# Softmax row sums in an attention kernel: five probability tiles summed by accumulating DMAs instead of by matrix multiplies

## The reference

```python
xn = _layernorm(x)                                  # x: (4, 2048, 512) float32
q = split(xn @ q_w.T + q_b) / sqrt(32)              # 16 heads of 32, per batch: 64 heads in all
k, v = split(xn @ k_w.T + k_b), split(xn @ v_w.T + v_b)
ctx = softmax(q @ k.T, axis=-1) @ v                 # scores of a head: 2048 x 2048
out = x + (ctx @ out_w.T + out_b) + tanh(xn @ weight @ aux_weight1 @ aux_weight2 + ffn_bias)
```

## Time and profile before

| | |
|---|---|
| median of 3 runs | 4641.23 us (4627.87 to 4641.38) |
| the profiled execution | 4647.09 us, its span 4645.3 us |
| busy share of the span | PE 98%, POOL 69%, DVE 63%, ACT 53% |
| granted PE clock, mean | 0.983 of full speed |
| DMA, 1000 to 4000 us | 20% of the 16 engines, 45 GB/s |

### The profile page before, as it was taken

One profiled execution on the slowest core, in us unless ns is written; L12 is line 12 of the kernel. 1 busy time (PEld: TensorE's weight loads), 2 busy tenths in 40 slices (PEclk: granted clock), 3 DMA queues, 4 the chain that ended last, 5 costly groups with the idle time before them and its releaser, 6 DMA issues.

```text
span 4645.3 us, 81083 instructions
## 1 busy us (share of the span) xinstructions
PE 4555.9 (98%) x23776; PEld 2481.1 (53%) x23776; DVE 2937.3 (63%) x4928; ACT 2460.2 (53%) x4517; POOL 3197.8 (69%) x863
## 2 busy tenths in 40 slices
PE   7999999999999999999999999999999999999999
PEld 5888888444444444444444444444444444444457
DVE  3434343777767776767676767777676767677524
ACT  1222221366666666666666666666666666666631
POOL 0222222588888888888888888888888888888830
PEclk9999999799999999999999999999999999999999
DMA  4444444211111111212211121111211222211157
GB/s 152 163 154 163 154 160 163 57 42 43 43 43 42 43 45 43 50 43 53 43 42 43 42 43 43 43 43 43 45 42 43 51 46 48 43 42 42 47 171 255
DMA packets 288290, 338.44 MB, mean 73 GB/s; under 512 B 169984, under 2 KB 171008, under 8 KB 275584
## 3 DMA queue, kind: packets, MB, share of 16 engines
q1 hardware_dynamic: 286384, 332.48, 26.3%
q10 hardware_dynamic: 1488, 0.79, 0.1%
HBM read 195.30 MB, written 137.36 MB: 72 GB/s over the span
## 4 chain that ended last, share of the span: by engine, by line
PE 76%; issue 3%; DVE 2%; ACT 1%; DMA 0%; ACTq 0%; DVEq 0%; SPq 0%
PE sm_bank L773 25%; PE st_bank L789 20%; PE pv_bank L795 20%; PE sum_bank L795 7%; PE sm_bank L190 3%; DVE part_max L714 2%; PE st_bank L190 1%; ACT probs L645 1%; PE sm_bank L782 0%; DMA q_stack<-max_row 0%; DVE k_stack L728 0%; DMA s_sums<-sum_copy 0%; DVE probs L736 0%; DMA sums_col<-s_sums 0%; ACT q_stack L663 0%
## 5 line engine op out<-in xcount | busy, mean ns | idle before, releaser
L714 DVE TENSOR_REDUCE part_max<-sm_bank 128x1 f32<-128x512 f32 x4096 | 2502.2, 682 | 904.4 <-PE sm_bank L773 903.8
L612 POOL TENSOR_TENSOR pool_sum<-pool_sum,probs 128x2048 f32<-128x2048 f32 x576 | 2637.0, 4578 | 474.1 <-ACT probs L645 451.0
L645 ACT ACTIVATE probs<-st_bank 128x512 f32<-128x512 f32 x4096 | 2183.0, 604 | 1102.3 <-PE st_bank L789 1065.2
L773 PE MATMUL sm_bank<-k_stack,q_stack 96*128 96x512 f32 x4096 | 1849.7, 455 | 38.7 <-issue 17.4
L789 PE MATMUL st_bank<-q_stack,k_stack 97*128 97x512 f32 x4096 | 1651.4, 404 | 15.2 <-ACT probs L645 11.0
L773 PEld LDWEIGHTS sm_bank<-k_stack,q_stack 96*128 96x128 f32 x4096 | 782.6, 191 | 990.9 <-DVE part_max L714 622.6
L795 PE MATMUL pv_bank<-probs,v_head 128*32 128x512 f32 x8192 | 1029.8, 603 | 0.0
L789 PEld LDWEIGHTS st_bank<-q_stack,k_stack 97*128 97x128 f32 x4096 | 783.4, 191 | 160.1 <-ACT probs L645 73.3
L795 PEld LDWEIGHTS pv_bank<-probs,v_head 128*32 128x32 f32 x8192 | 214.4, 109 | 494.1 <-issue 370.1
L612 POOL TENSOR_TENSOR pool_sum<-probs 128x2048 f32<-128x2048 f32 x64 | 293.4, 4585 | 143.5 <-ACT probs L645 143.5
L795 PE MATMUL sum_bank<-probs,ones_att 128*32 128x512 f32 x2560 | 338.1, 600 | 0.0
(11 more groups left out here) (84 smaller groups left out, 2034.7 us busy)
## 6 DMA issues: line engine op xcount, KB each, us to landing
q_stack<-s_q_hi SPq DMA_DIRECT2D x128, 256.0 KB, 4.6
k_stack<-s_k_hi SPq DMA_DIRECT2D x128, 256.0 KB, 6.1
x_in<-in_x SPq DMA_DIRECT2D x16, 1024.0 KB, 7.7
s_q_hi<-qk_hi SPq DMA_DIRECT2D x16, 1024.0 KB, 4.3
s_q_lo<-qk_lo SPq DMA_DIRECT2D x16, 1024.0 KB, 6.4
s_k_hi<-qk_hi SPq DMA_DIRECT2D x16, 1024.0 KB, 4.3
s_k_lo<-qk_lo SPq DMA_DIRECT2D x16, 1024.0 KB, 6.4
s_v<-v_out SPq DMA_DIRECT2D x16, 1024.0 KB, 4.3
```

Of the source, the lines that this page charges most:

```text
L612: nc.gpsimd.tensor_tensor(total[:], one[:], probs[kt % PROBS][:], ALU.add).then_inc(pool_added, 1)
L645: nc.scalar.activation(probs[kt % PROBS][:, q * BLK:(q + 1) * BLK], st_bank[:, st_place(kt * QB + q)], ACT.Exp, scale=SCALE).then_inc(prob ...
L714: nc.vector.tensor_reduce(part_max[:, k:k + 1], sm_bank[:, sm_place(sm_slot(k))], AX.X, ALU.max).then_inc(max_scores_read, 1)
L773: nc.tensor.matmul(sm_bank[:, sm_place(sm_slot(k))], q_st[r][0:ROWS, q * P:(q + 1) * P], k_st[r][0:ROWS, b * BLK:(b + 1) * BLK], start=Tru ...
```

## The change

The five tiles that PE summed become `DMA_TILES` 1, 4, 7, 10, 13. SP copies the first of them into a new SBUF tile `dma_sum` (`first_tile`), and POOL issues four DMAs that add the others to it in place (`join`, `accum_op=ALU.add`), after its adds 2, 4, 6 and 8; each waits until the one before has landed (`joined`). PE sums `dma_sum` and `pool_sum` with ones in `add_up`, once a head, after tile 5 of the next head (`CUT` 6, it was 4). The bank of the sums becomes one turn in the ring of the maxima, which has four banks (`SM_BANKS`). POOL's first add now takes tiles 0 and 2, and `scale` comes after the seventh add (`SCALE_ADD` 7, it was 6). `RECIP_UNIT` moves from 48 to 56.

```diff
-BANKS = 3
+SM_BANKS, ST_BANKS = 4, 3
-RECIP_UNIT = 48
-CUT = 4
-DIRECT = [2, 5, 8, 11, 14]
-POOL_TILES = [kt for kt in range(KT) if kt not in DIRECT]
+SUM_UNIT = 40
+RECIP_UNIT = 56
+CUT = 6
+DMA_TILES = [1, 4, 7, 10, 13]
+POOL_TILES = [kt for kt in range(KT) if kt not in DMA_TILES]
+JOINED = (len(DMA_TILES) - 1) * DMA
+JOIN_AFTER = {2: 1, 4: 2, 6: 3, 8: 4}
-SCALE_ADD = 6
+SCALE_ADD = 7
...
+SM_TURN = [*range(TURN_UNIT), "max", *range(TURN_UNIT, SUM_UNIT), "sum", *range(SUM_UNIT, UNITS), None, None]
...
+            def first_tile(h, r):
+                sp.wait_ge(probs_ready, PRIME + h * UNITS + QB * (DMA_TILES[0] + 1))
+                sp.dma_start(dma_sum[r % 2][:], probs[DMA_TILES[0] % PROBS][:]).then_inc(first_copied, DMA)
...
                 if more >= 1:
                     load_row(following, (r + 1) % GROUP)
+                    first_tile(following, (r + 1) % GROUP)
...
+            def join(h, r, j):
+                if j == 1:
+                    pool.wait_ge(first_copied, PRIME + h * DMA + DMA)
+                else:
+                    pool.wait_ge(joined, h * JOINED + (j - 1) * DMA)
+                pool.sem_inc(join_due, 1)
+                nc.gpsimd.dma_start(dma_sum[r % 2][:], probs[DMA_TILES[j] % PROBS][:],
+                                    accum_op=ALU.add).then_inc(joined, DMA)
...
+            def sum_up(h, r, i):
+                add(h, r, i)
+                if i in JOIN_AFTER:
+                    join(h, r, JOIN_AFTER[i])
...
                         if old in POOL_TILES:
                             act.wait_ge(pool_added, PRIME + h * POOL_ADDS - back * POOL_ADDS + adds_after(old))
+                        elif old == DMA_TILES[0]:
+                            act.wait_ge(first_copied, PRIME + h * DMA + DMA)
+                        elif not (back and isinstance(h, int) and h == 0):
+                            act.wait_ge(joined, h * JOINED - back * JOINED + DMA_TILES.index(old) * DMA)
...
-                last = spread(pv_bank, v_sb[r][:, kt], tile, kt == 0, kt == KT - 1)
-                if kt in DIRECT:
-                    if kt == DIRECT[0]:
-                        pe.wait_ge(sums_copied, PRIME + h)
-                    last = spread(sum_bank, ones[:], tile, kt == DIRECT[0], False)
-                last.then_inc(tile_used, 1)
-            def add_partial(h, r):
+                spread(pv_bank, v_sb[r][:, kt], tile, kt == 0, kt == KT - 1).then_inc(tile_used, 1)
+            def add_up(h, r, more):
+                if more >= 2:
+                    pe.wait_ge(max_scores_read, PRIME + h * UNITS + 2 * UNITS + sm_before("sum")[0] + 1)
+                pe.wait_ge(joined, h * JOINED + JOINED)
+                spread(sum_bank, ones[:], dma_sum[r % 2], True, False)
                 pe.wait_ge(pool_added, PRIME + h * POOL_ADDS + POOL_ADDS)
                 spread(sum_bank, ones[:], pool_sum[r % 2], False, True).then_inc(sums_ready, 1)
```

More of the change, by code:

```diff
@@ L38, with sm_place, sm_before @@
 AHEAD = 4
-TURN_SLOT = 8
-RECIP_UNIT = 48
-CUT = 4
-DIRECT = [2, 5, 8, 11, 14]
-POOL_TILES = [kt for kt in range(KT) if kt not in DIRECT]
+TURN_UNIT = 8
+SUM_UNIT = 40
[3 more added lines that the diff above has]
+POOL_TILES = [kt for kt in range(KT) if kt not in DMA_TILES]
 POOL_ADDS = len(POOL_TILES) - 1
-SCALE_ADD = 6
+JOINED = (len(DMA_TILES) - 1) * DMA
+JOIN_AFTER = {2: 1, 4: 2, 6: 3, 8: 4}
+SCALE_ADD = 7
+RESULT_TILES = [8, 9]
 PACK = SEQ // P
[L51 to L65, removed]
+SM_TURN = [*range(TURN_UNIT), "max", *range(TURN_UNIT, SUM_UNIT), "sum", *range(SUM_UNIT, UNITS), None, None]
+def sm_place(what):
+    return SM_TURN.index(what) % SM_BANKS
+def sm_before(what):
+    slot = SM_TURN.index(what) - SM_BANKS
+    while SM_TURN[slot] is None:
+        slot -= SM_BANKS
+    return SM_TURN[slot], int(slot < 0)
 def st_slot(u):
@@ L73, in st_place @@
 def st_place(u):
-    return st_slot(u) % BANKS
+    return st_slot(u) % ST_BANKS
 def st_units_before(u):
     return next(v for v in range(u - 1, u - UNITS, -1) if st_place(v % UNITS) == st_place(u)) + 1
-assert UNITS == 64 and sm_slot(UNITS - 1) == 64 and st_slot(UNITS - 1) == 65
+assert UNITS == 64 and len(SM_TURN) % SM_BANKS == 0 and st_slot(UNITS - 1) == 65
 def adds_after(kt):
@@ L443, in build_attend @@
         pool_sum = [sb(f"pool_sum{s}", [P, SEQ]) for s in range(2)]
+        dma_sum = [sb(f"dma_sum{s}", [P, SEQ]) for s in range(2)]
         ones, ident = sb("ones_att", [P, DH]), sb("ident_att", [P, P])
@@ L450, in build_attend @@
         ctx_out = [sb(f"ctx_out{s}", [P, BLK]) for s in range(2)]
[L451 to L452 removed]
+        st_bank = ps("st_bank", [P, ST_BANKS, BLK])
+        sm_bank = ps("sm_bank", [P, SM_BANKS, BLK])
         pv_bank = ps("pv_bank", [P, BLK])
[L454 removed]
+        sum_bank, turn_bank = sm_bank[:, sm_place("sum")], sm_bank[0:QT, sm_place("max"), 0:P]
         consts_ready, ident_zero = sem("consts_ready"), sem("ident_zero")
@@ L460, in build_attend @@
         row_max_ready, turned_ready, max_row_ready = sem("row_max_ready"), sem("max_turned"), sem("max_row_ready")
+        first_copied, join_due, joined = sem("first_copied"), sem("join_due"), sem("joined")
         pool_added, sums_ready, recip_ready, context_ready = sem("pool_added"), sem("sums_ready"), sem("recip_ready"), sem("context_ready")
@@ L470, in build_attend @@
         ctx_hi, ctx_lo = [tiled(q_st[2]), tiled(q_st[1])], [tiled(k_st[2]), tiled(k_st[1])]
-        res = [tiled(probs[DIRECT[2] % PROBS]), tiled(probs[DIRECT[3] % PROBS])]
-        out_banks = [sm_bank[:, 0], sm_bank[:, 1], sm_bank[:, 2], st_bank[:, 0]]
+        res = [tiled(probs[kt % PROBS]) for kt in RESULT_TILES]
+        out_banks = [sm_bank[:, b] for b in range(SM_BANKS) if b != sm_place("sum")] + [st_bank[:, 0]]
         assert len(out_banks) == JT and BLK == DIM
@@ L548, in _ @@
             load_row(0, 0)
+            first_tile(0, 0)
             def body(h, r, more, following):
@@ L627, in body @@
                     if more >= 1:
-                        add(following, (r + 1) % GROUP, i)
+                        sum_up(following, (r + 1) % GROUP, i)
             heads(pool, body)
@@ L707, in maxima @@
                 for k in range(UNITS):
-                    if k == TURN_SLOT and new:
+                    if k == TURN_UNIT and new:
                         negate(s - 1)
@@ L769, in max_scores @@
                     pe.wait_ge(head_loaded[r], PRIME + (s // GROUP) * (HEAD_DMAS * DMA) + HEAD_DMAS * DMA)
-                pe.wait_ge(max_scores_read, PRIME + s * UNITS + sm_units_before(k))
-                if k == TURN_SLOT + BANKS - 1:
+                old, back = sm_before(k)
+                if old == "max":
                     pe.wait_ge(max_row_ready, s)
-                nc.tensor.matmul(sm_bank[:, sm_place(sm_slot(k))], q_st[r][0:ROWS, q * P:(q + 1) * P],
+                elif old == "sum":
+                    pe.wait_ge(sums_copied, PRIME + s - 1)
+                else:
+                    pe.wait_ge(max_scores_read, PRIME + s * UNITS - back * UNITS + old + 1)
+                nc.tensor.matmul(sm_bank[:, sm_place(k)], q_st[r][0:ROWS, q * P:(q + 1) * P],
                                  k_st[r][0:ROWS, b * BLK:(b + 1) * BLK], start=True,
@@ L821, in both_scores @@
                     s, ahead, k0 = following + 1, 2, PER_TILE * (kt - KT + AHEAD)
-                if k0 == TURN_SLOT and more >= 1:
+                if k0 == TURN_UNIT and more >= 1:
                     turn_max(following, more >= 2)
@@ L859, in body @@
                             use(following, r1, 2 * p - 1)
-                        if p == 1:
-                            add_partial(h, r)
+                        if p == CUT // 2 - 1:
+                            add_up(h, r, more)
                 else:
@@ L877, in _ @@
             output(0, 0, True)
-            add_partial(ALL_HEADS - 1, (ALL_HEADS - 1) % GROUP)
+            add_up(ALL_HEADS - 1, (ALL_HEADS - 1) % GROUP, 0)
             output(1, 1, True)
```

16 lines of the change are left out of this document (9 added, 7 removed).

## The result

The changed kernel takes 5301.7 us, the median of 4 runs (5287.84 to 5317.11); the kernel before, run beside it, takes 4637.59 (4627.87 to 4641.38). The ratio is 1.1435, 95% interval 1.1402 to 1.1467: slower by 14%. The forecast was 5041, with a range of 4400 to 5490, and slower the likeliest. The profiled execution took 5287.84 us, its span 5286.1, with a mean granted clock of 0.892 in place of 0.983.

A forecast was written before the change was run, and what follows sets the result against it. PE bound the kernel before at 55.84 us a head; a hidden loop through POOL's scale and SP's queue would take over, 8.7 + 32.5 + 1.3 + 3.0 + 13.0 + 1.0 + 3.0 = 62.5, over 60 heads 5041 us, range 4400 to 5490.

The forecast's parts named there:

- What the prediction said would show it right: PE idle near 10 us for the row, clock 0.50 after, POOL waiting only before its first add, rows 62.5 apart.
- scores to first add (1): From the start of a head's scores to POOL's first add, now on tile 2: 8.7 us, 5.1 before.
- the clock (6): PE idles for the row each head, so its first burst runs at half clock: 3.0 us, ends nothing and 4.9.
- adds, scale, three issues (2, 3): POOL's order up to the scale's end: seven adds 32.5 us, scale 1.3, three accumulating DMA issues at 1.0 each, 3.0.
- scale to row and scores (4): SP's queue from the scale's end through store and loads until the row lands: 13.0 us, range from 8.2.
- contention (5): The third accumulating DMA, sent just before the scale, meets the loads: 1.0 us, between nothing and 4.3.
- most of it moves before the loads start: Why the third accumulating DMA's meeting with the loads was put at 1.0 us, not a 1 MB transfer's 4.3.
- The loop's turn: The program loop's turn every fourth head: 1.0 us on PE's mean head, 47.4 to 48.4; none added to the 62.5.
- rival of slow accumulating DMAs: Landings of 13 us make the second and third join wait 3.7 each: 69.9 us a head, 5485 us; chance 0.13.
- rival of the short loop: In SP's queue the row passes the load, issues cost 0.4, clock stays: 51.9 us a head, 4407 us; chance 0.19.
- PE as the bound (4182): PE stays the bound and the change does what its parts suggest: 48.4 us a head, 4182 us; chance 0.06.

The follow-up runs named there:

- x1: The changed kernel with the maxima's row of the head after next sent ahead of the context's store and the loads in SP's queue: 4587.67 us, ratio 0.9892.
- x5: The changed kernel with the maxima's row of the head after next put between the context's store and the seven loads: 4567.84 us, ratio 0.9892.
- x3: The kernel before with only SCALE_ADD 8 in place of 6, so POOL's scale stands two adds later: 5241.42 us, ratio 1.1292.
- x4: The changed kernel without its four accumulating DMAs a head and their waits, the copy of tile 1 kept: 4841.77 us, ratio 1.0442.
- x8: The changed kernel with the row ahead of store and loads, and tile 1's copy issued from ACT after tile 2's exponentials: 4642.92 us, ratio 1.0035.
- x9: The changed kernel with the row ahead of store and loads, and the seven loads moved behind the load of the sums' column: 4614.25 us, ratio 0.9951.
- x10: The changed kernel with only the seven loads moved, behind the load of the sums' column; the row stays behind scale and store: 4757.18 us, ratio 1.0268.

## Why the prediction held, and where its sizes were off

The direction and the mechanism were right: PE's work shrank and the time rose, because the loop through POOL's adds, the scale, the store, the loads and the row came to stand above PE. x1 takes the scale, the store and the loads out of it, x5 the loads, and the time fell below before; x3 builds it without the change. What the prediction said would show it right is there: PE waits 13.37 for the row, the clock is 0.50 behind it, POOL waits for ACT before its first add and within the head for 0.17 only. Between waits PE's pieces are as said, from the chain of the changed kernel:

```profile
2141.58 0.43 PE sm_bank L811
...
2145.51 1.85 PE pv_bank L833 x16
2147.36 0.43 PE sm_bank L811
```

A pair of tiles takes 5.78, a burst with its way to the next work 3.93, where 3.85 was forecast. The gain on PE is real and unused.

By its terms, for this head:

| term | forecast | measured |
|---|---|---|
| scores to first add (1) with the clock (6) | 11.7 | 10.5 |
| adds, scale, three issues (2, 3) | 36.8 | 36.4 |
| scale to row and scores (4) with contention (5) | 14.0 | 17.5 |
| sum | 62.5 | 64.4 |

The sum is closer than its terms: the clock and the issues were put too high, which hides part of what contention was put too low.

*Contention* was the mis-sized term: 1.0 forecast, and 17.5 - 12.6 = 4.9 against x4, which has the same order without the accumulating DMAs; term 4 itself held, 12.6 (x4) and 12.7 (x3) for 13.0. The step that failed was "most of it moves before the loads start", worked out from a landing like that of a plain transfer, 4.3, and from DMA engines at 20%. An adding DMA takes 7.9, so the third one, issued at 2164.92 just ahead of the scale, is under way while the store and most of the loads are issued. And the fourth one, which the prediction left out, is issued at 2176.15, 1.0 after the row. The four stores are issued in 4.00 where it was 1.83 and is 1.83 in x4: 2.2 of the 4.9. The row comes 9.5 after its issue began (2184.63 - 2175.17) where x4 has 6.7: the other 2.8. No run parts the third DMA from the fourth in these 2.8. The row's long issue, a median of 5.06 where it was 1.01, is not contention: it is 4.99 in x3 and 4.98 in x4, where no accumulating DMA runs and the row is issued right behind the last load. Of the row's landing of 10.1, 6.6 (x3) and 6.7 (x4) come with that place alone.

*The clock* was put too high, at 3.0: half clock lasts from 2184.63 to somewhat before 2190, and the scores reach the first add in 10.5, where x5 at full clock takes 8.5 and term 1 had 8.7: 2.0. *The issues* were put at 1.0 each: POOL goes on 0.62 after the start of one, and x4 makes the three 1.7 to 2.5 instead of 3.0. The Trainium skill, in "DMA: Bandwidth & Descriptors", section "Specifications", gives some 1 us to the first byte of a DMA issued from GpSimd. No run here shows the first byte; the row shows that POOL was free for its next instruction after 0.62.

*The loop's turn* was assumed hidden. It is not: the first 60 intervals of the row have a mean of 66.24 (870.3 to 4844.4), 1.85 above the head shown, and from 2130.76 on three heads in a row took 64.4, 72.0 and 68.3, the second of them with the turn in it. PE and DVE stop at the turn, and the loop has no slack in which to take that up.

Of the missing 241 us (641 measured, 400 forecast), 60 x 1.9 = 114 are the terms, 60 x 1.85 = 111 what the other heads take beyond the one shown, the turn above all, and 13 the last three intervals, which were counted at 55.84 each and took 180.8 together.

The rival of slow accumulating DMAs (13 us a landing, joins waiting) fell: the slowest landing was 11.5, and no join waited. The Trainium skill, in "Collectives: The Full Stack", section "The bandwidth ceiling: the fold count and why AG ≠ RS ≠ AR", puts the collective that adds (ReduceScatter) at half the rate of the one that copies (AllGather), since the add reads two sources. Here the ratio is 7.0 / 4.3 = 1.6 between the quickest landings, and 7.9 / 4.9 = 1.6 between the medians: for one DMA inside SBUF the direction agrees, and the size is smaller. The rival of the short loop had its place right and its premise wrong: the row did not pass the loads, but when x5 lets it, the time is below before. PE as the bound (4182) was not reached by any version. x5, the fastest, still had the DMAs and what is left of the loop.

## What to carry to other kernels

When one engine is at 98%, look for the loop that runs just behind it: an in-order queue that holds a late store, then large loads, then a small transfer that somebody waits for, closes such a loop, and work taken off the full engine can bring it out. Work each candidate loop out as a sum over its engines and queues before work is moved onto any of them. Here the small transfer on the critical path belonged ahead of the large loads in its queue; this one move, with no change of the computation, turned 14% slower into 1% faster (x5, 4567.84).

## What was not expected of the hardware

- A DMA of 1 MB that adds in SBUF lands in 7.9 us (median of 256), the same DMA as a plain copy in 4.9; and in the chains of x1, x5, x8 and x9, where the loads of a head or the copy of tile 1 are under way beside it, it took 11.3 to 12.7. It holds POOL for 0.62 to the start of the next instruction, and as a plain copy it is recorded with 0.58 instead of 0.87.
- The added DMAs stretched some transfers and left others alone (medians): the store of the context landed in 1.6 before and 4.3 now, the four that spread the ratios in 2.0 and 6.1, but the loads of 256 KB in 4.6 and 4.7 (`s_q_hi`) and in 7.1 and 7.2 (`s_v`). The transfer of the reciprocals, 1.4 in the changed kernel, took 6.1 behind the loads (x10).
- A small DMA issued right behind the seven loads holds SP for 5.0 (x3 and x4, with no accumulating DMA), and the same one issued ahead of them for 0.6 (x5).
- DVE stands for some 6 us once every fourth head, at the turn of the program's loop: in x1 13 such waits and 78.5 us between 1000 and 4000 us.
- The granted clock went from 1.00 to 0.50 (2.4 to 1.2 GHz) in the middle of PE's wait for the row, while POOL and the DMA engines were busy. Behind the wait of 2.05 in x5 it stayed at 1.00.
